# Delta rule on TensorE: square sums as 64x64 products, gate projections after the second T products, diagonal ahead of the cross products

## The chip, the cores and the metric

The kernel runs on one core of one Trainium2 chip. The core has TensorE for matrix products (PE in the profile, its weight loads PEld), VectorE (DVE), ScalarE (ACT), GpSimd (POOL) and SyncE (SP), which issues transfers. Each has its own instruction stream, and they meet through semaphores. All data is fp32, and each product of the program is two matmul records in the trace. The metric is device time in microseconds of the whole program, median of the runs.

## The reference, cut to what matters

The network is eight stages on an input of 8 x 512 x 128. The change is in one of them, the gated delta rule, with 16 heads of 64 channels:

```python
q = (h @ q_w).reshape(bsz, seq, H, DK)      # k and v alike
q = q / (jnp.linalg.norm(q, axis=-1, keepdims=True) + EPS)
k = k / (jnp.linalg.norm(k, axis=-1, keepdims=True) + EPS)
alpha = jax.nn.sigmoid(h @ alpha_w + alpha_b).reshape(bsz, seq, H, DK)
beta = jax.nn.sigmoid(h @ beta_w + beta_b)
def step(s, inp):
    qt, kt, vt, at, bt = inp
    s = s * at[..., None]
    u = jnp.einsum('bhd,bhdv->bhv', kt, s)
    s = s + bt[..., None, None] * (kt[..., None] * (vt - u)[..., None, :])
    out = jnp.einsum('bhdv,bhd->bhv', s, qt)
    return (s, out)
y = y * jax.lax.rsqrt(jnp.mean(y * y, axis=-1, keepdims=True) + EPS) * head_norm_w
```

The square sums of the change are the sums over a head's 64 channels: of q and k for their norms, of y for the last line.

## The kernel before

`stage_delta` works on one batch row and one pair of heads at a time: 8 rows by 8 pairs are 64 steps, and a 65th drains what is behind. Head 0 of a pair lies on partitions 0 to 63, head 1 on 64 to 127. The 512 tokens of a row are 8 chunks of 64. Within a chunk the recurrence is solved by doubling: a triangular matrix T is built over six levels (diagonal blocks of 1, 2, 4, up to 32 tokens, and then the cross blocks between two chunks), and between pairs of chunks a state S is carried.

A step is pipelined over its neighbours. While T of one step is built, the projections, norms and gates of the next step run in between, and so do the output and head norm of the step before. The order is written out by hand for each engine. TensorE has it in `step()` (line 2911), thirteen times in a row in the body of a loop that runs five times:

- `gram(0)`, `cross_z`, `cross_t`, `diagonal`, `gram(1)`, then `solve(0)`, `state_and_output(0)`, `from_state(1)`;
- for the levels 1 to 5: `z_and_gram(l)` (the Z products of level l on two quarters of the array, and the gram products of level l+1 on the other two), VectorE and ScalarE copy one half of Z each (`z_copy`), then `t_step(l)`, and ScalarE copies T (`t_copy`);
- in between `solve(t)`, `state_and_output(t)`, `from_state(t)` for the chunk pairs 1 to 3. ScalarE copies U after each `solve`, and VectorE makes S (`state`) between `state_and_output` and `from_state`;
- of the next step: `project_qk` after `t_step(1)`, `square_sums` after `z_and_gram(2)`, `project_gates` after `z_and_gram(3)`, `key_norms` after `z_and_gram(4)`, `project_v`; of the step before: `head_sums` after `t_step(4)` and `output` after `z_and_gram(5)`.

`square_sums` (line 2839) takes eight products over the whole array: a 128x128 block of squares is the stationary operand and a 128x2 head mask moves. `head_sums` does the same with four.

VectorE has, in its order: `z_copy`, `masked(3)`, `residual(2)`, `sums_in`, `transposed(2)`, `z_copy` of level 3, `norms` (three small operations on the 16 sums, after GpSimd's root), and only then `state(2)`. GpSimd has the gates' multiplications: `carry(l)` multiplies kd and k of level l by tails of alpha and releases `lv_ready`, for which `gram` and `z_and_gram` wait; `roots` is a power of 0.5 over the 16 sums. `gram(1)` waits besides for `gr_free`, which VectorE gives after it has read the gram products of level 0 (`masked(0)`).

Banks of PSUM: Q_ and K_ take the projections, X_ takes the square sums, the diagonal, the key scales and the keys by tokens (`ket`), in turn.

Of the kernel before, what the change touches and what calls it, by code (L numbers as in the profile page):

```python
# [8 lines left out]
ALU = mybir.AluOpType  # L9
# [7 lines left out]
P = 128  # L17
# [2461 lines left out]
def stage_delta(core):  # L2479
# [89 lines left out]
    with nc.Block() as block_:  # L2569
# [12 lines left out]
        def _(g):  # L2582
# [67 lines left out]
            with g.Fori(0, LAST + 1) as i:  # L2650
                ch.reset()
                g.wait_ge(k_free, 1)
                g.sem_clear(k_free)
                carry_k(0, kn)
                carry_kq(0, kd, kdn).then_inc(lv_ready, 1)
# [24 lines left out]
                g.tensor_copy(tH[:], tails(LEVELS + 1)).then_inc(kd_free, 1)  # L2680
# [4 lines left out]
        def _(pe):  # L2685
# [185 lines left out]
            def head_sums():  # L2871
# [38 lines left out]
            pe.sem_inc(out_ps, 1)  # L2910
            def step():
# [52 lines left out]
        def _(a):  # L2964
# [3 lines left out]
            a.sem_inc(ket_ready, 1)  # L2968
# [49 lines left out]
            with a.Fori(0, LAST + 1) as i:  # L3018
                a.wait_ge(kd_free, 1)
# [663 lines left out]
```

## Time and profile before

| | us |
|---|---|
| median of 3 runs | 5245.73 |
| lowest, highest | 5245.05, 5253.82 |
| the profiled execution | 5255.62 |
| its span, from the first to the last instruction | 5253.4 |
| of it, the delta stage's steps | about 1494 to 4005 |
| TensorE busy in the span | 4061.1 (77%) |
| VectorE, ScalarE, GpSimd busy | 2979.3, 1785.2, 2663.1 |

Times of the trace are read from the span's start. A step is measured here from one `e_ZX` copy on ScalarE to the next, since that copy occurs once in each. The share of TensorE's clock that was granted stands in the column PEclk: 1.00 is 2.4 GHz and 0.50 is 1.2 GHz. Matmuls are pipelined, so a group of them ends some 0.1 to 0.2 us after the next one has begun, and what a group costs TensorE is the time from its start to the next one's.

### The profile page before, as it was taken

The page shows a single profiled execution, that of the slowest core. Times are in us where ns is not written, and L with a number is a line of the kernel's source. Part 1 is how long each engine was busy: PE and PEld are TensorE (multiplying, and loading weights), DVE is VectorE, ACT ScalarE, POOL GpSimd, SP SyncE. Part 2 cuts the span into 40 slices and gives each one's busy share as a digit, 9 for nine tenths or more (in the row PEclk, how much of TensorE's full clock was granted, in tenths as well). Part 3 has the DMA queues.
Part 4 walks back from the last instruction along what each step waited for, and adds up shares of the span by engine and source line. Part 5 has one row for each costly group of instructions (what it writes and reads, how often), then busy time and mean ns, then how long its engine had stood idle before and what let it go on. Part 6 is the DMA issues. An engine that isn't in the chain of part 4 may idle for free. (4 is left out here: it accounts for less than half of the span.)

```text
span 5253.4 us, 171720 instructions
## 1 busy us (share of the span) xinstructions
PE 4061.1 (77%) x68604; PEld 3253.1 (62%) x68604; DVE 2979.3 (57%) x8041; ACT 1785.2 (34%) x4061; POOL 2663.1 (51%) x3000
## 2 busy tenths in 40 slices
PE   4679964664179888889898898889897769588685
PEld 2434444553157777777777777767775469577685
DVE  5832277655645655656556565555565554488723
ACT  4722232442023333333333333333333135311163
POOL 2310017514456665666666566666664251377644
PEclk8989986786579998999999999999998879799797
DMA  0030004653000000000000000000000056300154
GB/s 22 3 135 0 0 4 127 184 168 105 15 17 10 13 11 10 13 10 13 11 10 13 11 11 13 11 12 11 11 13 11 1 184 237 109 1 1 58 185 123
DMA packets 129671, 248.79 MB, mean 47 GB/s; under 512 B 24672, under 2 KB 60657, under 8 KB 127345
## 3 DMA queue, kind: packets, MB, share of 16 engines
q1 hardware_dynamic: 98224, 178.93, 10.8%
q0 software_dynamic: 16384, 33.59, 2.2%
q10 hardware_dynamic: 14400, 26.22, 1.4%
q8 instruction: 565, 9.26, 0.7%
q14 instruction: 98, 0.80, 0.0%
HBM read 178.89 MB, written 59.77 MB: 45 GB/s over the span
## 5 line engine op out<-in xcount | busy, mean ns | idle before, releaser
L2596 POOL TENSOR_TENSOR e_kd<-e_kd,e_tail 128x512 f32<-128x512 f32 x325 | 369.1, 1136 | 575.3 <-PE psum L2703 562.8
L2733 PE MATMUL psum<-e_T,e_N 64*64 64x32 f32 x10400 | 403.4, 231 | 65.3 <-remote 63.2
L2733 PEld LDWEIGHTS psum<-e_T,e_N 64*64 64x64 f32 x10400 | 367.3, 147 | 117.9 <-issue 110.5
L2703 PE MATMUL psum<-e_kd,e_k 64*64 64x64 f32 x10400 | 415.7, 235 | 2.3 <-issue 1.7
L729 POOL DMA_INDIRECT m_back<-m_rows_out,m_idx x256 | 254.4, 994 | 302.0 <-DVEq L1169 127.8
L2703 PEld LDWEIGHTS psum<-e_kd,e_k 64*64 64x64 f32 x10400 | 368.3, 147 | 7.3 <-issue 1.1
L723 POOL DMA_INDIRECT rows_in<-xn,m_idx x256 | 256.2, 1001 | 146.2 <-issue 76.2
L2754 PE MATMUL psum<-e_Z,e_TT 64*64 64x32 f32 x8320 | 302.2, 223 | 28.8 <-DVE e_Z L3106 22.6
L840 PE MATMUL psum<-m_rowsT,m_w 128*128 128x128 f32 x2304 | 319.2, 298 | 3.1 <-DVE m_h L1145 2.3
L840 PEld LDWEIGHTS psum<-m_rowsT,m_w 128*128 128x128 f32 x2304 | 306.7, 214 | 5.0 <-DVE m_h L1145 2.3
L3106 DVE COPY e_Z<-psum 64x256 f32<-64x256 f32 x325 | 135.8, 418 | 305.8 <-PE psum L2733 305.6
L2754 PEld LDWEIGHTS psum<-e_Z,e_TT 64*64 64x64 f32 x8320 | 273.7, 137 | 51.3 <-issue 37.8
L2998 ACT ACTIVATE e_T<-psum 128x256 f32<-128x256 f32 x325 | 125.9, 387 | 522.2 <-PE psum L2754 522.2
L856 PE MATMUL psum<-m_wd,m_h 128*128 x1856 | 256.9, 283 | 34.2 <-DVE m_out L1157 31.5
L2590 POOL TENSOR_TENSOR e_k<-e_k,e_tail 128x256 f32<-128x256 f32 x390 | 276.8, 710 | 0.0
L856 PEld LDWEIGHTS psum<-m_wd,m_h 128*128 128x128 f32 x1856 | 235.6, 199 | 39.9 <-issue 39.8
L3005 ACT ACTIVATE e_Z<-psum 64x256 f32<-64x256 f32 x325 | 123.9, 381 | 314.5 <-PE psum L2733 312.9
L384 PE MATMUL psum<-f_hid,f_h 128*128 128x512 f32 x512 | 223.1, 594 | 2.2 <-remote 2.2
L2612 POOL TENSOR_TENSOR e_ssb<-e_ssb,e_half_power 128x16 f32<-128x16 f32 x66 | 191.4, 2899 | 35.6 <-DVE e_ssb L3146 35.6
L818 PE MATMUL psum<-ident,m_rows 128*128 128x128 f32 x400 | 73.5, 314 | 174.8 <-issue 116.0
L3100 DVE COPY_PREDICATED e_AT<-e_lowi,psum 128x256 f32<-128x256 int32 x390 | 205.6, 527 | 0.0
L3113 DVE STREAM_TRANSPOSE e_TT<-e_T 128x512 f32<-128x512 f32 x195 | 138.3, 709 | 102.5 <-ACTq L2999 100.5
(460 smaller groups left out, 10849.6 us busy)
## 6 DMA issues: line engine op xcount, KB each, us to landing
m_w<-in_m_w SPq DMA_DIRECT2D x88, 516.0 KB, 5.8
m_w<-in_m_w SPq DMA_DIRECT2D x224, 129.0 KB, 2.3
m_rows<-rows_in SPq DMA_DIRECT2D x100, 256.0 KB, 3.8
m_rows_out<-m_out ACTq DMA_DIRECT2D x100, 256.0 KB, 2.1
m_w<-in_m_w SPq DMA_DIRECT2D x88, 259.0 KB, 3.7
e_w<-in_e_w SPq DMA_DIRECT2D x66, 321.0 KB, 2.9
rows_in<-xn SPq DMA_DIRECT2D x6, 2048.0 KB, 23.7
m_wd<-in_m_wd SPq DMA_DIRECT2D x3, 2048.0 KB, 8.2
```

The lines of the kernel that those rows point to most:

```text
L384: r = pe.matmul(c.ps[m][:], w[:, k, m * P:(m + 1) * P], hid[n][:, k, :], start=(k == 0), stop=(k == HC - 1))
L723: g.indirect_dma_start(out=xs[i], out_offset=bass.IndirectOffsetOnAxis(ap=idx[i][:, n, k:k + 1], axis=0), in_=y2[:, pl.b0[i] * TB + n, :], ...
L729: g.indirect_dma_start(out=back[:, n, k, :], out_offset=None, in_=os[i], in_offset=bass.IndirectOffsetOnAxis(ap=idx[i][:, n, k:k + 1], axi ...
L840: r = pe.matmul(c.ps[2 * (u % 2) + i][:, cols(j)], w[:, k % WR * BPS + j, n:n + P], xgT[:, k % 2, cols(j)], start=True, stop=True)
L856: r = pe.matmul(c.ps[Y_][:, t * P:(t + 1) * P], h[:, u % DEPTH, t * P:(t + 1) * P], wd[:, bass.ds(experts[0][t // TPB], 1), m * D:(m + 1) ...
L2590: return g.tensor_tensor(even(k[:], m), even(src[:], m), gate, ALU.mult)
L2596: return g.tensor_tensor(both_odd(dst[:], m), both_odd(src[:], m), gate.unsqueeze(1).broadcast_to((P, 2, nb, m)), ALU.mult)
L2612: g.tensor_tensor(flat_ss, flat_ss, half_power[:], ALU.pow).then_inc(root_ready, 1)
L2703: r = pe.matmul(c.psum[half(h), G_, chunk(u)], keys[half(h), chunk(u)], both_odd(gated[half(h), :, chunk(u)], 1 << l), start=True, stop=True)
L2733: r = pe.matmul(c.psum[half(1 - h), Z_, u * HC:(u + 1) * HC], N[half(h), l - 1, chunk(u)], even(T[half(h), chunk(u)], 1 << l), start=True, ...
L2754: r = pe.matmul(even(c.psum[half(h), T_, chunk(u)], 1 << l), left[half(h), chunk(u)], Z[half(h), u, :], start=False, stop=False, skip_grou ...
L3100: return lambda: v.copy_predicated(cols(AT[:]), wide(lowi[:, l, :]), gr[:, :, 1]).then_inc(gr_free, 1)
```

## The change

Four things are moved or rewritten, all in `stage_delta`.

1. `sums_by_head` makes the square sums out of 64x64 products on all four quarters of the array: 32 of them in place of 8 for q and k, 16 in place of 4 for y. The two quarters on the diagonal write to bank X_, the two off it to bank K_, and VectorE adds the two banks: one more small operation in `sums_in` and one more for y. After it has read K_ it gives `sums_read`, for which TensorE waits before it writes K_ again.
2. `project_gates` moves from behind `z_and_gram(3)` to behind `t_step(2)`, ahead of `solve(2)`, and waits for `sums_read` between its two products.
3. `diagonal` goes ahead of `cross_t`. It writes X_, which ScalarE must have read: the copy of `ket` moves from the end of ScalarE's step to the start of the next, behind the copy of k, and the copy of kd moves ahead of the copy of ZX.
4. GpSimd multiplies kd of level 0 first, behind a new semaphore `kd_read` and no longer behind ScalarE's copy of k, and k of level 0 second.

```diff
+            def sums_by_head(of, at, t, done):
+                for bank, other in ((X_, 0), (K_, 1)):
+                    for h in range(2):
+                        a = 1 - h if other else h
+                        r = pe.matmul(c.psum[half(a), bank, 2 * at:2 * at + 2], of[half(h), chunk(2 * t + a)], hm[half(h), :],
+                                      start=True, stop=True)
+                        if done:
+                            r.then_inc(done, 1)
...
-                        at = 2 * (n * TB + t)
-                        r = pe.matmul(c.ps[X_][:, at:at + 2], sq[:, n, block(t)], hm[:], start=True, stop=True)
-                r.then_inc(ss_ps, 1)
+                        sums_by_head(sq[:, n, :], n * TB + t, t, ss_ps if n * TB + t + 1 == 2 * TB else None)
...
-                for n in range(2):
-                    r = pe.matmul(c.ps[Q_ + n][:], W[:, (2 + n) * P:(3 + n) * P], hs[:], start=True, stop=True)
-                r.then_inc(ab_ps, 1)
+                pe.matmul(c.ps[Q_][:], W[:, 2 * P:3 * P], hs[:], start=True, stop=True)
+                pe.wait_ge(sums_read, 1)
+                pe.sem_clear(sums_read)
+                pe.matmul(c.ps[K_][:], W[:, 3 * P:4 * P], hs[:], start=True, stop=True).then_inc(ab_ps, 1)
...
                 for t in range(TB):
-                    r = pe.matmul(c.ps[X_][:, 2 * t:2 * t + 2], ysq[:, block(t)], hm[:], start=True, stop=True)
-                r.then_inc(sy_ps, 1)
+                    sums_by_head(ysq, t, t, sy_ps if t + 1 == TB else None)
 
             def output():
 
+                pe.wait_ge(sums_read, 1)
+                pe.sem_clear(sums_read)
...
-                v.wait_ge(ss_ps, 1)
+                v.wait_ge(ss_ps, 4)
                 v.sem_clear(ss_ps)
-                v.tensor_copy(ssb[:].rearrange("p n t h -> p (n t h)"), c.ps[X_][:, 0:4 * TB]).then_inc(ss_ready, 1)
+                ch.link(v.tensor_copy(sums[:], c.ps[K_][:, 0:4 * TB]))
+                v.sem_inc(sums_read, 1)
+                v.tensor_tensor(ssb[:].rearrange("p n t h -> p (n t h)"), sums[:], c.ps[X_][:, 0:4 * TB], ALU.add).then_inc(ss_ready, 1)
```

On TensorE at the start of a step, `e_T,e_NA` is `cross_z`, `e_TTH,e_ZX` is `cross_t`, `e_kqn,e_kn` is `diagonal` and `e_kd,e_k` is `gram(1)`. Before:

```order
L2764 MATMUL psum<-e_T,e_NA 64x64 x8
L2770 ISA
L2772 ISA
L2775 MATMUL psum<-e_TTH,e_ZX 64x64 x8
L2693 ISA
L2696 MATMUL psum<-e_kqn,e_kn 64x64 x16
L2920 ISA
L2922 ISA
L2709 ISA
L2703 MATMUL psum<-e_kd,e_k 64x64 x16
```

Changed:

```order
L2770 MATMUL psum<-e_T,e_NA 64x64 x8
L2699 ISA
L2702 MATMUL psum<-e_kqn,e_kn 64x64 x16
L2776 ISA
L2778 ISA
L2781 MATMUL psum<-e_TTH,e_ZX 64x64 x8
L2937 ISA
L2939 ISA
L2715 ISA
L2709 MATMUL psum<-e_kd,e_k 64x64 x16
```

The two waits of `cross_t` (the ISA rows ahead of it) now stand behind the diagonal.

On TensorE in the middle of a step, from the square sums (`e_headmask,e_sq`) on; `e_Z,e_TT` is `t_step(2)`, `e_hs,e_w` are the gate projections, `e_bv,..` is `solve(2)` and `e_T,e_N` begins `z_and_gram(3)`. Before:

```order
L2846 MATMUL psum<-e_headmask,e_sq 128x2 x8
L2747 ISA x2
L2750 ISA
L2754 MATMUL psum<-e_Z,e_TT 64x8x4 x16
L2786 ISA
L2788 MATMUL psum<-e_bv,e_TTH 64x64 x2
L2790 MATMUL psum<-e_bv,e_TX 64x64 x2
L2792 MATMUL psum<-e_bv,e_TTH 64x64 x2
L2724 ISA
...
L2703 MATMUL psum<-e_kd,e_k 64x64 x2
L2852 MATMUL psum<-e_hs,e_w 128x512 x2
```

Changed:

```order
L2849 MATMUL psum<-e_headmask,e_sq 64x2 x32
L2753 ISA x2
L2756 ISA
L2760 MATMUL psum<-e_Z,e_TT 64x8x4 x16
L2864 MATMUL psum<-e_hs,e_w 128x512
L2866 ISA
L2867 MATMUL psum<-e_hs,e_w 128x512
L2792 ISA
L2794 MATMUL psum<-e_bv,e_TTH 64x64 x2
L2796 MATMUL psum<-e_bv,e_TX 64x64 x2
L2798 MATMUL psum<-e_bv,e_TTH 64x64 x2
L2730 ISA
```

The gate projections stood behind all of `z_and_gram(3)`, and stand ahead of `solve(2)` now.

On GpSimd at the start of a step, where `e_al` is alpha. Before:

```order
L2653 ISA
L2590 TENSOR_TENSOR e_k<-e_kn,e_al 128x256
L2596 TENSOR_TENSOR e_kd<-e_kdn,e_al 128x512
L2656 COPY e_tail<-e_tailn 128x512
```

Changed:

```order
L2654 ISA
L2597 TENSOR_TENSOR e_kd<-e_kdn,e_al 128x512
L2657 ISA
L2591 TENSOR_TENSOR e_k<-e_kn,e_al 128x256
L2659 COPY e_tail<-e_tailn 128x512
```

The wait for ScalarE's copy of k stood ahead of both multiplications, and stands between them now.

## Rows read from the trace of the kernel before

**Rows 1.** One tile's instructions, ScalarE's ZX copy: min/median/max ns, first and last start

```profile
L3024 ACT ACTIVATE e_ZX<-psum x65: 384/384/386, 1494.0 to 3969.1; 128x256 f32<-128x256 f32 x65
```

**Rows 2.** Five single steps by windows: length, busy by engine, PEclk, DMA share, GB/s

```profile
3121.94:3157.95 36.01, 32.34 (x848) 26.45 (x848) 22.93 (x53) 13.99 (x31) 24.06 (x30) 1.00 0.05 12
3351.40:3388.80 37.40, 33.69 (x848) 27.57 (x848) 22.68 (x53) 13.99 (x32) 24.58 (x30) 0.95 0.05 11
3044.67:3083.27 38.60, 34.98 (x848) 28.02 (x848) 22.65 (x53) 13.99 (x32) 24.11 (x30) 0.91 0.04 11
3194.97:3235.72 40.75, 36.18 (x848) 28.33 (x848) 22.69 (x53) 13.99 (x32) 24.71 (x30) 0.92 0.04 11
1955.68:2001.06 45.38, 37.02 (x848) 29.46 (x848) 23.00 (x54) 13.97 (x31) 26.62 (x32) 0.88 0.04 10
```

**Rows 3.** Windows inside one step, ahead of the clock's fall and behind it

```profile
3082.00:3099.20 17.20, 14.90 (x388) 12.22 (x385) 11.18 (x30) 5.95 (x13) 9.12 (x11) 1.00 0.01 3
3099.20:3106.10 6.90, 6.69 (x110) 4.91 (x107) 2.70 (x6) 0.66 (x2) 4.56 (x3) 0.51 0.01 2
```

**Rows 4.** Timeline of TensorE around that fall: start us, length us, what

```profile
3097.08 1.95 PE L2846 MATMUL psum<-e_headmask,e_sq 128*128 128x2 f32 x16
3098.95 1.68 PE L2754 MATMUL psum<-e_Z,e_TT 64*64 64x32 f32 x32
...
3103.45 3.29 PE L2852 MATMUL psum<-e_hs,e_w 128*128 128x512 f32 x4
```

**Rows 5.** Timeline of TensorE in the undisturbed step of 36.01 us

```profile
3122.59 0.68 PE L2775 MATMUL psum<-e_TTH,e_ZX 64*64 64x64 f32 x16 [0.79 <-DVE e_TTH L3117]
3123.11 1.10 PE L2696 MATMUL psum<-e_kqn,e_kn 64*64 64x64 f32 x32
3124.20 1.15 PE L2703 MATMUL psum<-e_kd,e_k 64*64 64x64 f32 x32
...
3135.69 1.95 PE L2846 MATMUL psum<-e_headmask,e_sq 128*128 128x2 f32 x16
3137.57 1.12 PE L2754 MATMUL psum<-e_Z,e_TT 64*64 64x32 f32 x32
...
3139.59 0.25 PE L2733 MATMUL psum<-e_T,e_N 64*64 64x32 f32 x2 [0.52 <-remote]
...
3140.68 1.98 PE L2852 MATMUL psum<-e_hs,e_w 128*128 128x512 f32 x4
...
3143.70 0.45 PE L2822 MATMUL psum<-e_S,e_kdH 64*64 64x64 f32 x8 [0.32 <-DVE e_S L3125]
...
3151.09 1.05 PE L2878 MATMUL psum<-e_headmask,e_ysq 128*128 128x2 f32 x8
...
3152.15 0.25 PE L2733 MATMUL psum<-e_T,e_N 64*64 64x32 f32 x2
```

**Rows 6.** Timeline of VectorE in the same step

```profile
3122.90 0.73 DVE L3100 COPY_PREDICATED e_AT<-e_lowi,psum 128x256 f32<-128x256 int32 x1
...
3140.88 0.42 DVE L3106 COPY e_Z<-psum 64x256 f32<-64x256 f32 x1 [0.80 <-PE psum L2733]
3141.33 0.78 DVE L3152 TENSOR_SCALAR e_ssb<-e_ssb 128x16 f32<-128x16 f32 x1
3142.15 0.55 DVE L3154 SCALAR_TENSOR_TENSOR e_rq<-e_ssb 128x8 f32<-128x8 f32 x1
3142.62 0.19 DVE L3155 RECIPROCAL e_rk<-e_ssb 128x8 f32<-128x8 f32 x1
3143.26 0.28 DVE L3125 SCALAR_TENSOR_TENSOR e_S<-e_S,e_tH,psum 128x64 f32<-128x64 f32 x1 [0.46 <-PE psum L2802]
```

**Rows 7.** Timeline of GpSimd in the same step

```profile
3122.43 1.50 POOL L2596 TENSOR_TENSOR e_kd<-e_kdn,e_al 128x512 f32<-128x512 f32 x1
...
3138.13 2.90 POOL L2612 TENSOR_TENSOR e_ssb<-e_ssb,e_half_power 128x16 f32<-128x16 f32 x1 [0.41 <-DVE e_ssb L3146]
```

**Rows 8.** Timeline of ScalarE in the same step

```profile
3151.38 0.38 ACT L2998 ACTIVATE e_T<-psum 128x256 f32<-128x256 f32 x1 [1.14 <-PE psum L2754]
```

More of the change, by code:

```diff
@@ L2515, in stage_delta @@
     rq = [st.sb(f"rq{n}", [P, 2 * TB]) for n in range(3)]
-    su = st.sb("su", [P, TB, 2])
+    su, sums = st.sb("su", [P, TB, 2]), st.sb("sums", [P, 4 * TB])
     w_ready, w_free, hs_ready, hs_free = s("w_ready"), s("w_free"), s("hs_ready"), s("hs_free")
     qk_ps, sq_ready, ss_ps, ss_ready, root_ready = s("qk_ps"), s("sq_ready"), s("ss_ps"), s("ss_ready"), s("root_ready")
+    sums_read = s("sums_read")
     rk_ready, rk_ps, ab_ps, al_ready, be_ready = s("rk_ready"), s("rk_ps"), s("ab_ps"), s("alpha_ready"), s("beta_ready")
@@ L2651, in _ @@
                 ch.reset()
+                g.wait_ge(kd_read, 1)
+                g.sem_clear(kd_read)
+                carry_kq(0, kd, kdn)
                 g.wait_ge(k_free, 1)
                 g.sem_clear(k_free)
-                carry_k(0, kn)
-                carry_kq(0, kd, kdn).then_inc(lv_ready, 1)
+                carry_k(0, kn).then_inc(lv_ready, 1)
                 ch.link(g.tensor_copy(tail[:], tailn[:]))
@@ L2679, in _ @@
                 carry_kq(LEVELS, kdH, kd).then_inc(kdh_done, 1)
-                g.tensor_copy(tH[:], tails(LEVELS + 1)).then_inc(kd_free, 1)
+                ch.link(g.tensor_copy(tH[:], tails(LEVELS + 1)))
+                g.sem_inc(kd_free, 1)
+            g.wait_ge(kd_read, 1)
+            g.sem_clear(kd_read)
             g.wait_ge(hs_free, 1)
@@ L2910, in _ @@
             pe.sem_inc(out_ps, 1)
+            pe.sem_inc(ke_ps, 1)
             def step():
@@ L2916, in step @@
                 cross_z()
+                diagonal()
                 cross_t()
-                diagonal()
                 pe.wait_ge(even_ready, 1)
@@ L3018, in _ @@
             with a.Fori(0, LAST + 1) as i:
+                a.wait_ge(ke_ps, 1)
+                a.sem_clear(ke_ps)
+                a.activation(odd(k[:], 1), odd(kn[:], 1), ACT.Copy).then_inc(k_free, 1)
+                a.activation(flat(ket), c.ps[X_][:], ACT.Copy).then_inc(ket_ready, 1)
                 a.wait_ge(kd_free, 1)
                 a.sem_clear(kd_free)
-                a.activation(odd(k[:], 1), odd(kn[:], 1), ACT.Copy).then_inc(k_free, 1)
+                a.activation(both_even(kd[:], 1), both_even(kdn[:], 1), ACT.Copy).then_inc(even_ready, 1)
                 a.wait_ge(zx_ps, 1)
@@ L3061, in _ @@
                 t_copy(5)
[L3062 to L3064 removed]
+            a.wait_ge(ke_ps, 1)
+            a.sem_clear(ke_ps)
             a.wait_ge(kd_free, 1)
             a.sem_clear(kd_free)
+            a.sem_inc(ket_ready, 1)
         @block_.vector
@@ L3238, in _ @@
                 values(i + 1)
-                v.wait_ge(sy_ps, 1)
+                v.wait_ge(sy_ps, 4)
                 v.sem_clear(sy_ps)
-                v.scalar_tensor_tensor(su[:].rearrange("p t h -> p (t h)"), c.ps[X_][:, 0:2 * TB], 1.0 / DH, rq[0][:],
-                                       ALU.mult, ALU.add).then_inc(su_ready, 1)
+                ch.link(v.scalar_tensor_tensor(sums[:, 0:2 * TB], c.ps[K_][:, 0:2 * TB], 1.0 / DH, rq[0][:], ALU.mult, ALU.add))
+                v.sem_inc(sums_read, 1)
+                v.scalar_tensor_tensor(su[:].rearrange("p t h -> p (t h)"), c.ps[X_][:, 0:2 * TB], 1.0 / DH,
+                                       sums[:, 0:2 * TB], ALU.mult, ALU.add).then_inc(su_ready, 1)
                 transposed(4)
```

12 lines of the change are left out of this document (4 added, 8 removed).

## Prediction

> **What bounds the kernel now.** The change touches only the delta stage, so I read how long one of its 65 steps takes and how much that varies. The first and the last ZX copy [rows 1] are 3969.1 - 1494.0 = 2475.1 us apart, 64 steps of 38.67 us on average. The windows over single steps [rows 2] show three kinds. A step whose granted clock is 1.00 takes 36.01 us, one in which the clock is low for a while 37.40, one in which it is low for twice as long 38.60; rarer are one with two falls (40.75) and the step in which the loop jumps back (45.38, 6.8 more than 38.60; there are four of these, 27 us, and I leave them as they are). Without them the mean is 38.67 - 27 / 64 = 38.25, so 2.24 us of an average step is the low clock.
>
> In the undisturbed step TensorE is busy for 32.34 of 36.01 us, and VectorE for 22.93, ScalarE for 13.99, GpSimd for 24.06 [rows 2]: TensorE bounds it, and what isn't TensorE's own work is a row of short waits of 0.3 to 0.8 us [rows 5]. The clock falls behind the square sums [rows 3, 4]. Up to 3099.20 it is granted in full, although the 16 records that move two columns each have just run for 1.95 us without a gap; then it is 0.51 for 6.9 us, the second T products take 1.68 instead of 1.12, and the gate projections 3.29 instead of 1.98 [rows 4, 5]. TensorE was not idle before the fall, it was doing little per unit of time.
>
> The Trainium skill ("TensorE: Matmul & The Clock Gate", "Why this matters for your kernels") ties the fall to idle gaps between bursts of matmuls. The rows above show a fall with TensorE busy throughout, so here the trace does not follow that reading.
>
> **Start of the step (parts 3 and 4).** Today `cross_t` waits 0.79 us for the ZX copy, `diagonal` follows, and `gram(1)` starts at 3124.20 [rows 5]. That start is GpSimd's doing: its kd of level 0 ends at 3122.43 + 1.50 = 3123.93 [rows 7]. The change puts the diagonal into the wait, so that TensorE could be 0.79 earlier, and takes GpSimd out of last place, since the 1.50 us multiplication no longer waits for ScalarE. Next in line is `gr_free`: VectorE's masked copy of level 0 ends at 3122.90 + 0.73 = 3123.63 [rows 6], nothing in the change moves it, and from a VectorE end to the product that waits takes 0.16 (S ends at 3143.54, `from_state` starts at 3143.70 [rows 5, 6]). So `gram(1)` starts at 3123.79: **0.4 us** gained of the 0.79. The copies moved on ScalarE fill its idle time ahead of ZX; if they made ZX late, that would fall behind the diagonal (1.10 us).
>
> **Square sums (part 1).** Today 16 records take 3137.57 - 3135.69 = 1.88 us. Afterwards they are 64 records on four quarters with two columns moving. The trace has no such group. The nearest is `z_and_gram`, 64 records on four quarters with 32 or 64 columns moving: 3140.68 - 3139.59 = 1.09 us [rows 5]. The bounds: no cheaper than half of that if the columns counted, no dearer than today's 1.88. I take 1.09, for the same number of 64x64 weight loads: gain **0.79 us**, range 0 to 1.3. The extra addition on VectorE costs at most 0.2 us (the smallest operation there is 0.19 [rows 6]) and lies ahead of GpSimd's root, which starts 0.5 us earlier or more anyway because the sums do.
>
> By the Trainium skill ("TensorE: Matmul & The Clock Gate", "LDWEIGHTS") a load takes its columns over 1.2 per ns, 53 ns for 64; sixteen in each quarter would be an estimated 0.85 us, and the gain 1.03 instead of 0.79. In the rows `z_and_gram` takes 1.09, and the rows decide.
>
> **Gate projections (part 2).** They add nothing; they move. They now cover the wait for the copy of T, 0.52 us ahead of `z_and_gram(3)` [rows 5], and `sums_read` between them costs nothing, since VectorE reads the sums during the T products (1.12). But they covered something where they stood: with 1.98 us between `z_and_gram(3)` and `state_and_output(2)` VectorE had time for its Z copy and the norms before `state(2)`. Follow this in the clean step. `z_and_gram(3)` starts at 3139.59 - 0.40 - 0.79 - 0.52 + 1.98 = 3139.86, so 0.27 later than today. VectorE's Z copy starts 1.29 behind it (3140.88 - 3139.59 [rows 5, 6]): 3141.15 to 3141.57. The norms take 1.48 (3141.33 to 3142.81 [rows 6]) to 3143.08; the root they need takes 2.90 on GpSimd and ends at 3141.03 today [rows 7], earlier afterwards. S takes 0.28, and `from_state(3)` starts at about 3143.55, where it starts at 3143.70 today [rows 5]. Of 1.71 us gained up to there **0.15** is left; `state_and_output(2)` comes 1.98 sooner after `z_and_gram(3)` than it did, and TensorE stands idle for about 2 us behind it, waiting for S. With roundings in my favour (0.1 us less for the square sums, which need no change of tiling behind them) it may be 0.25.
>
> **Head sums.** Eight records at 1.05 become 32 records, by the same rate half of 1.09. `z_and_gram(5)`, next, starts today at 3152.15, which is also when T is there: its copy ends at 3151.38 + 0.38 = 3151.76 [rows 8], and 0.39 from T copy to product is what it takes. So of 0.5 us at most 0.1 counts. `output` now waits for `sums_read`, covered by `z_and_gram(5)`.
>
> **Sum, clock apart.** 0.15 to 0.35 us a step, I take 0.3, times 64 is 19 us.
>
> **The clock.** 2.24 us a step is at stake, 143 us in all. In favour: the thin stretch shrinks from 1.88 to 1.09 us; and a fall behind it would now spend about 2 of its 6.9 us on idle time, where a halved clock costs nothing: 2.24 x 2 / 6.9 = 0.65 us. Against: the idle stretch is itself a new place at which the clock may fall. I take half of the 0.65, 0.35 us a step, 22 us. Together 41 us: the profiled execution's 5255.62 becomes 5215. It lies 9.9 over the median of the runs, so for the median I say 5245.7 - 41 = **5205**.
>
> **The rivals.**
> - *The clock hardly falls any more.* With the thin stretch cut nearly in half most steps run at 35.7 (36.01 - 0.3), a third with a fall of 1.4 (37.40 - 36.01 [rows 2]): 36.2. That is 38.25 - 36.2 = 2.05 x 64 = 131 us at best and half of that if every step keeps one short fall (37.1: 74 us). Middle: 5143. For: undisturbed steps exist today with the long thin stretch. Against: the new idle stretch. 0.2.
> - *The stall takes it all.* `from_state(3)` starts where it did, the falls stay as they are: 5235 to 5256. For: my own sum leaves 0.15 of 1.71. 0.13.
> - *Slower: a second fall in each step.* The 2 us of idle TensorE behind `state_and_output(2)` bring the clock down besides the fall behind the square sums. A step with two falls costs 40.75 - 36.01 = 4.74 [rows 2]; at about 4 a step takes 35.7 + 4 = 39.7, 1.45 x 64 = 93 us more: 5338; if it happens in every third step, 5270. It decides once the low clock costs over 2.54 us a step. Against: waits of 0.8 us pass without a fall [rows 5], but none of 2 us is in the rows. 0.1. The page of the Trainium skill cited above, on idle gaps, speaks for this rival.
> - *Slower: two-column products don't gain from the quarters.* If 64 small records take 1.88 again, `z_and_gram(3)` starts 1.06 later than today, `from_state(3)` 0.6: 0.5 x 64 = 32 us slower, 5275. It decides from 1.5 us. Against: `z_and_gram`. 0.07.
>
> **How the numbers follow.** My forecast, 5190 to 5230, has 0.5. Below it lies the clock rival (0.2), above it the stall (0.13), the two slower ones (0.17). The range 5125 to 5270 leaves out the best of the first and most of the slower ones, about 0.17. A measurement tells 0.2% apart, 10.5 us: faster 0.5 + 0.2 and a little of the stall rival: 0.73; same 0.11; slower 0.16.
>
> **What would show it.** In the changed profile: `diagonal` straight behind `cross_z`, and `gram(1)` 0.4 earlier against ZX, released by VectorE. 64 square sum records in 1.0 to 1.1 us; 1.5 or more makes that step wrong. An idle time of about 2 us ahead of `from_state(3)`, released by VectorE's S, with the three norm operations straight ahead of it. Undisturbed steps of 35.6 to 35.8; under 35.3 would mean that the stall is smaller than I reckon, over 36.0 that it is larger. And the spread: the share of steps with a low clock, whether it falls behind the square sums or behind the idle stretch. A PEclk of 0.94 in the stage as a whole would mean no gain from the clock, and if it went under 0.9, the prediction is wrong in sign.

## The result, and the profile after

| | before | after |
|---|---|---|
| median of 4 runs each, us | 5245.39 | 5305.01 |
| lowest, highest | 5236.94, 5253.82 | 5300.68, 5310.45 |
| the profiled execution | 5255.62 | 5310.45 |
| 64 steps of the delta stage | 2475.1 | 2524.95 |
| an undisturbed step | 36.0 | 35.4 |

The ratio is 1.0114, 95% interval 1.0095 to 1.0133: 60 us slower, where 41 us faster was forecast. The two profiled executions are 55 us apart, and 50 of these lie in the 64 steps. Windows over the stage and over single steps (length; busy time and instructions of PE, PEld, DVE, ACT, POOL; PEclk, DMA share, GB/s), first the stage before:

```profile
1494.00:3969.10 2475.10, 2206.07 (x54272) 1787.33 (x54272) 1452.37 (x3328) 895.12 (x1984) 1559.78 (x1854) 0.94 0.04 11
```

and then the changed kernel, its stage and four of its steps [rows 2]:

```profile
1499.14:4024.09 2524.95, 2125.72 (x58886) 1714.12 (x58884) 1424.78 (x3457) 883.45 (x1985) 1530.47 (x1855) 0.92 0.04 11
2948.86:2984.25 35.39, 30.32 (x927) 25.05 (x924) 22.14 (x55) 13.80 (x32) 23.92 (x30) 1.00 0.05 13
2791.91:2829.52 37.61, 31.88 (x927) 25.91 (x924) 22.24 (x55) 13.80 (x32) 23.95 (x30) 0.95 0.04 12
2829.52:2868.23 38.71, 31.95 (x928) 25.48 (x924) 22.22 (x55) 13.80 (x32) 23.91 (x30) 0.96 0.04 11
3069.11:3112.47 43.36, 36.57 (x928) 28.96 (x924) 22.35 (x55) 13.83 (x32) 23.98 (x30) 0.84 0.04 11
```

TensorE has 80 us less work in the stage, the undisturbed step is 0.6 us shorter, and the stage is longer all the same. So the loss is in what disturbs the steps. One part of that are falls of the granted clock to half. The clock record says how often: stretches at half clock, called low clock from here on, add up to 315 us before and 399 after (PEclk 0.94 and 0.92 are the same thing: 1 - 315 / (2 x 2475) and 1 - 399 / (2 x 2525)). 7 of 64 steps had two falls before, 20 have two or more now, and 4 have none, where 11 had.

TensorE in the undisturbed step [rows 5], from its timeline (start, length, line, tiles, idle time before it and who ended it):

```profile
2948.65 1.03 PE L2702 MATMUL psum<-e_kqn,e_kn 64*64 64x64 f32 x29
2949.52 0.68 PE L2781 MATMUL psum<-e_TTH,e_ZX 64*64 64x64 f32 x16
2950.71 1.15 PE L2709 MATMUL psum<-e_kd,e_k 64*64 64x64 f32 x32 [0.51 <-DVE e_AT L3120]
...
2961.24 0.25 PE L2739 MATMUL psum<-e_T,e_N 64*64 64x32 f32 x2
...
2962.19 1.09 PE L2849 MATMUL psum<-e_headmask,e_sq 64*64 64x2 f32 x64
2963.24 1.12 PE L2760 MATMUL psum<-e_Z,e_TT 64*64 64x32 f32 x32
2964.30 1.12 PE L2864 MATMUL psum<-e_hs,e_w 128*128 128x512 f32 x2
2965.26 1.02 PE L2867 MATMUL psum<-e_hs,e_w 128*128 128x512 f32 x2
...
2970.29 0.45 PE L2828 MATMUL psum<-e_S,e_kdH 64*64 64x64 f32 x8 [2.02 <-DVE e_S L3145]
...
2973.85 1.08 PE L2874 MATMUL psum<-e_sq,e_ones 128*64 128x512 f32 x4
...
2977.35 0.63 PE L2849 MATMUL psum<-e_headmask,e_ysq 64*64 64x2 f32 x30
```

The diagonal fills the wait for ZX, `gram(1)` starts 1.85 us behind ZX in place of 2.26 and is released by VectorE, and the square sums take 1.05 us up to the next group. And there is an idle stretch of 2.02 us ahead of `from_state(3)`. VectorE in that stretch [rows 6]:

```profile
2967.80 0.42 DVE L3126 COPY e_Z<-psum 64x256 f32<-64x256 f32 x1 [2.04 <-PE psum L2739]
2968.25 0.78 DVE L3174 TENSOR_SCALAR e_ssb<-e_ssb 128x16 f32<-128x16 f32 x1
2969.06 0.54 DVE L3176 SCALAR_TENSOR_TENSOR e_rq<-e_ssb 128x8 f32<-128x8 f32 x1
2969.53 0.19 DVE L3177 RECIPROCAL e_rk<-e_ssb 128x8 f32<-128x8 f32 x1
2969.86 0.28 DVE L3145 SCALAR_TENSOR_TENSOR e_S<-e_S,e_tH,psum 128x64 f32<-128x64 f32 x1
```

The three norm operations stand between the Z copy and S, and TensorE waits for S.

**What comes behind the idle stretch.** The step of 37.61 us by windows: up to 2816.30, the 3.4 us behind that, and TensorE's idle stretch by itself:

```profile
2791.91:2816.30 24.39, 19.50 (x569) 15.31 (x564) 15.30 (x41) 6.60 (x16) 15.25 (x18) 1.00 0.01 3
2816.30:2819.70 3.40, 3.02 (x68) 2.10 (x68) 1.19 (x3) 1.76 (x4) 2.04 (x6) 0.50 0.00 0
2812.14:2814.16 2.02, 0.00 (x0) 0.01 (x1) 1.85 (x5) 0.00 (x0) 2.02 (x3) 1.00 0.00 0
```

TensorE idles until 2814.16 and the clock halves at 2816.3. Where in a step do the falls begin? Before, 51 falls began behind the square sums (between 12 and 21.7 us after ZX) and none behind `from_state(3)` (21.7 to 29.5 us). Now 32 begin behind the sums and 45 behind `from_state(3)`. The others, 9 before and 5 now, begin 9.7 to 10.8 us after ZX or past 37.

**What happens to the square sums.** In the step of 38.71 us they read otherwise:

```profile
2842.83 0.57 PE L2849 MATMUL psum<-e_headmask,e_sq 64*64 64x2 f32 x27
2845.01 0.65 PE L2849 MATMUL psum<-e_headmask,e_sq 64*64 64x2 f32 x33 [1.61 <-issue]
2845.53 1.12 PE L2760 MATMUL psum<-e_Z,e_TT 64*64 64x32 f32 x32
```

TensorE stops in the middle of a group whose operands are all there, for 1.61 us, and "issue" says that nothing in the profile was waited for. The line's own page counts what this costs in the whole program, in the matmul queue:

```profile
L2849 PE MATMUL psum<-e_headmask,e_sq x4224: 161/194/262, 1480.0 to 4040.2; 64*64 64x2 f32 x192
...
  issue: 49.9, 30
```

30 pauses and 49.9 us; 29 of them fall into the 64 steps. Before, the 66 groups had one such wait (3.8 us). The pauses have an order: in each of the three whole passes of the loop that I counted, they fall into the steps 1, 3, 6, 8, 10 and 12 of the 13, and all pauses inside groups of small products, these and others, fall on TensorE's instruction number 242 or 243 modulo 256, counted from the loop's start (matmuls, weight loads and semaphore instructions as recorded). The kernel before has such pauses as well, at 82 to 85 modulo 256, but only 4.3 us of them in 13 steps, where the changed kernel has 14.6. The instruction queue's row of the DMA section over the stage, before and after:

```profile
q8 instruction: 448, 7.34, 1.3%
```

```profile
q8 instruction: 481, 7.88, 1.3%
```

A packet is 7.34 MB / 448 = 16.4 KB. The loop body of 13 steps is 22880 and 24780 recorded TensorE instructions, so the 64 steps of these windows are 440 and 477 times 256, against 448 and 481 packets. So nearly all of this queue is TensorE's program, 256 instructions in a packet. Around the pause above the DMA view of 2841 to 2845, 40 slices of 0.1 us, shows one packet:

```profile
GB/s 0 0 0 0 0 0 0 0 0 0 0 0 0 0 0 0 0 164 0 0 0 0 0 0 0 0 0 0 0 0 0 0 0 0 0 0 0 0 0 0
...
q8 instruction: 1, 0.02, 1.5%
```

It moves at 2842.7, and the group goes on at 2845.01. The other pauses look the same: the changed kernel has 60 pauses of over 0.25 us inside groups of equal products between its first and last ZX copy, and each ends 2.2 to 2.9 us after the start of the packet before it, while the packets come 5.1 us apart in the median. From the start of `z_and_gram(2)` to the end of the quarter sums TensorE uses up 256 instructions (64 products and 64 weight loads each) in 2.0 us (2961.24 to 2963.24 in the undisturbed step), less than these 2.2 to 2.9 us from packet to instruction.

### The profile page after: what moved, and what is told of

Same layout as the page of the kernel before. It is cut to its first block and busy times, and to the rows that moved or that the text cites. A ratio compares the mean times of both kernels' runs of the same rounds, so it can differ in the third digit from the quotient of the medians.

```text
span 5308.5 us, 181702 instructions
## 1 busy us (share of the span) xinstructions
PE 3979.9 (75%) x73332; PEld 3179.5 (60%) x73332; DVE 2952.3 (56%) x8172; ACT 1773.6 (33%) x4061; POOL 2630.0 (50%) x3000
## 5 line engine op out<-in xcount | busy, mean ns | idle before, releaser
L2760 PE MATMUL psum<-e_Z,e_TT 64*64 64x32 f32 x8320 | 315.8, 227 | 36.1 <-DVE e_Z L3126 21.1
L2760 PEld LDWEIGHTS psum<-e_Z,e_TT 64*64 64x64 f32 x8320 | 290.2, 143 | 54.5 <-issue 46.4
L2591 POOL TENSOR_TENSOR e_k<-e_k,e_tail 128x256 f32<-128x256 f32 x390 | 253.9, 651 | 0.0
L2828 PE MATMUL psum<-e_S,e_kdH 64*64 64x64 f32 x1560 | 89.2, 233 | 171.8 <-DVE e_S L3145 171.8
L3028 ACT ACTIVATE e_U<-psum 128x128 f32<-128x128 f32 x260 | 71.7, 276 | 402.3 <-PE psum L2798 389.9
```

The costliest lines, as they stand in the source:

```text
L2591: return g.tensor_tensor(even(k[:], m), even(src[:], m), gate, ALU.mult)
L2760: r = pe.matmul(even(c.psum[half(h), T_, chunk(u)], 1 << l), left[half(h), chunk(u)], Z[half(h), u, :], start=False, stop=False, skip_grou ...
```

## The experiments

Each kernel is the changed kernel with one edit, unless it says otherwise. Low clock is the sum of half-clock stretches in the 64 steps, in us; pauses are those inside groups, in us per 13 steps. A ratio is against the kernel before on the same chip.

| run | ratio, 95% interval | 64 steps, us | shortest step | low clock | pauses |
|---|---|---|---|---|---|
| kernel before | 1 | 2475 | 35.99 | 315 | 4.3 |
| changed kernel | 1.0114 (1.0095, 1.0133) | 2525 | 35.37 | 399 | 14.6 |
| e1_full_sums | 1.0052 (1.0038, 1.0065) | 2489 | 37.14 | 332 | 2.3 |
| e2_sums_only | 0.9996 (0.9981, 1.0011) | 2471 | 35.50 | 266 | 15.5 |
| e3_start_only | 0.9892 (0.9868, 0.9915) | 2402 | 35.44 | 246 | 2.5 |
| e4_norms_late | 0.9829 (0.9805, 0.9854) | 2377 | 34.45 | 192 | 13.4 |
| e6_fill_aligned | 0.9838 (0.9816, 0.9859) | 2383 | 35.19 | 85 | 7.8 |
| e7_fill_drift | 0.9960 (0.9945, 0.9976) | 2434 | 35.61 | 144 | 13.3 |
| e8_full_norms_late | 0.9830 (0.9808, 0.9852) | 2383 | 34.98 | 201 | 3.1 |
| e9_norms_late_unroll65 | 0.9843 (0.9814, 0.9872) | 2387 | 34.45 | 188 | 15.8 |
| e10_wide_norms_late | 0.9735 (0.9713, 0.9757) | 2332 | 34.40 | 69 | 14.5 |
| e11_wide_only | 1.0022 (1.0006, 1.0037) | 2474 | 35.47 | 294 | 13.3 |
| e12_full_wide_norms_late | 0.9734 (0.9717, 0.9752) | 2318 | 35.16 | 45 | 2.8 |
| e13_before_wide | 0.9830 (0.9809, 0.9851) | 2373 | 35.99 | 59 | 3.2 |
| e14_shift128 | 1.0124 (1.0095, 1.0152) | 2545 | 35.43 | 403 | 15.1 |
| e15_shift64 | 1.0150 (1.0133, 1.0168) | 2556 | 35.36 | 413 | 16.2 |

The last three ran on chips on which the kernel before takes 5586.41 (e13) and 5563.56 us (e14, e15). Their traces reach the first of the 64 steps at 1635 to 1643 us, where the others do at 1480 to 1500, so much of what is longer there lies ahead of the delta stage, and only ratios and stage times compare with the rest. Stage, low clock and pauses come from one profiled execution each; that of e12 took 5081.22 us, 22 below its median.

A shortest step isn't always an undisturbed one. e1's is its only step without low clock and holds a pause of 1.16 us, so without it 36.0:

```profile
2233.77 0.32 PE L2798 MATMUL psum<-e_bv,e_TTH 64*64 64x64 f32 x2 [1.16 <-issue]
```

e6's follows a step of 41.9 us, and e8's and e12's are the first of the stage; the next shortest without low clock take 35.46, 35.18 and 35.29.

**Taking the change apart.** e1 puts the full-array sums back and leaves parts 2 to 4; e2 is the kernel before with part 1 alone; e3 is the kernel before with parts 3 and 4 alone.

```diff
-                        sums_by_head(sq[:, n, :], n * TB + t, t, ss_ps if n * TB + t + 1 == 2 * TB else None)
+                        at = 2 * (n * TB + t)
+                        r = pe.matmul(c.ps[X_][:, at:at + 2], sq[:, n, block(t)], hm[:], start=True, stop=True)
```

> The changed kernel with the square sums and head sums as full-array products again (part 1 undone; gates, diagonal and GpSimd order as changed). Theory A (TensorE starves for instructions: in the changed kernel pauses of 0.6 to 2 us stand at every recorded index 242 modulo 256 that falls into dense small products, 15 us per 13 steps, against 3 to 5 us before): without the 64-record groups the long pauses inside the sums go, pauses fall to under 5 us per 13 steps, undisturbed steps get longer (about 36.0 to 36.4, since the sums take 1.88 and the norms stall behind z_and_gram(3) stays), and the time is 5240 to 5275, faster than the changed kernel's 5305. Theory B (the 2 us idle stretch ahead of from_state(3) lowers the clock and is the whole loss): the idle stretch stays, so low-clock time stays near 400 us and the time stays at 5300 or rises to 5330.

> The kernel before with part 1 alone (square sums and head sums on quarters of the array, gates, diagonal and GpSimd order as before). Theory A (starving for instructions): pauses of 1 to 2 us inside or behind the 64-record group in 4 to 7 of 13 steps, all at one index modulo 256; undisturbed steps about 35.3 to 35.6, mean step 38.5 to 39.3, time 5240 to 5290. Theory B (idle stretch): no 2 us idle ahead of from_state(3) here, so the group's 0.8 us is pure gain: 5190 to 5215.

> The kernel before with parts 3 and 4 alone (diagonal ahead of the cross products, GpSimd's kd first). Both theories: gram(1) 0.4 us earlier in each step, nothing else new: undisturbed steps 35.6, about 25 us faster than before, 5220, as long as pauses at block ends stay at 3 to 5 us per 13 steps. If the time is over 5240, the 0.4 us is taken back by the clock or by new places of the pauses.

Measured medians: 5272.34, 5239.92 and 5186.87 us, the kernel before 5240.35. e1 lies in theory A's range and e2 at its lower edge, both outside theory B's. Part 1 alone is worth nothing: the shortest step is 0.49 us shorter, and the pauses go from 4.3 to 15.5 us in 13 steps, 0.86 us a step. Parts 3 and 4 alone are worth 53 us, more than the 25 expected. From e3 to e1 only the gate projections move: 85 us slower, low clock 246 to 332, and the undisturbed step goes from 35.44 to about 36.0. 55 of e1's falls begin behind `from_state(3)`, where e3 has none. So part 2 as written costs about 35 us in the step, and 86 us more of low clock, which cost at most 43, are most of the rest. From e1 to the changed kernel the quarter sums come on top: 33 us slower.

**The idle stretch.** e4 puts VectorE's norms behind `residual(3)`, so that S no longer stands behind them. e6 leaves them and puts 35 small products of no use into the idle stretch (their result is overwritten), so many that a step has 2048 instructions and the packets' bounds lie at the same places in each; e7 puts 24, and the bounds go on drifting.

```diff
-                norms()
                 ...
                 residual(3)
+                norms()
```

```diff
+            def fill(n):
+
+                for j in range(n):
+                    h = j % 2
+                    pe.matmul(c.psum[half(h), O_, 3 * P:3 * P + DH], eye[half(h), :], eye[half(h), :], start=True, stop=True,
+                              skip_group_check=True)
...
                 z_and_gram(3)
                 state_and_output(2)
+                fill(35 + extra)
                 from_state(3)
```

(`extra` is 6 in the first of 13 steps and 0 in the others.)

> The changed kernel with VectorE's three norm operations moved from ahead of state(2) to behind residual(3). Theory B (idle stretch): the 2 us idle ahead of from_state(3) shrinks to under 0.5, key_norms waits up to 1 us more, undisturbed steps 34.6 to 35.0, low-clock time falls from 400 to under 330 us, time about 5215 to 5250. Theory A: pauses at index 242 modulo 256 stay at about 15 us per 13 steps, and the time gains only what the undisturbed step gains, 0.5 us a step: 5265 to 5285.

> The changed kernel with 35 more 64x64 products (140 instructions, six more once per 13 steps; their result is overwritten and unused) between state_and_output(2) and from_state(3), where TensorE idles for 2 us. A step becomes 2048 instructions, so that the ends of 256-instruction blocks fall at the same places in every step, one of them inside z_and_gram(2), none inside the square sums. Both causes are taken away: theory A expects pauses of under 4 us per 13 steps instead of 15; theory B expects no fall of the clock behind the idle stretch, low-clock time under 250 us instead of 400. The stall itself stays, undisturbed steps 35.4 to 35.6. Both right: 5150 to 5200. Only A right: about 5255. Only B right: about 5230.

> As the aligned one, but with 24 added products (96 instructions), so that block ends drift by 46 instructions a step and still fall into the square sums in some steps. Theory A: pauses of 8 to 16 us per 13 steps remain, the time lies 25 to 50 us above the aligned kernel. Theory B: the clock behaves as in the aligned kernel (under 270 us of low clock). If the two kernels come out alike, the pauses don't matter.

Measured: e4 5161.73, e6 5163.44, e7 5226.84 us. e4 in TensorE's timeline of its shortest kind of step, and VectorE ahead of it:

```profile
2890.22 0.45 PE L2828 MATMUL psum<-e_S,e_kdH 64*64 64x64 f32 x8 [0.41 <-DVE e_S L3145]
```

```profile
2889.33 0.42 DVE L3126 COPY e_Z<-psum 64x256 f32<-64x256 f32 x1 [2.04 <-PE psum L2739]
2889.78 0.28 DVE L3145 SCALAR_TENSOR_TENSOR e_S<-e_S,e_tH,psum 128x64 f32<-128x64 f32 x1
```

The idle time goes from 2.02 to 0.41 us, the shortest step from 35.37 to 34.45, and the falls behind `from_state(3)` from 45 to none. 0.92 x 64 = 59 us is the shorter step, and the other 84 of the 143 us gained come with the low clock, 399 to 192 us, and some 6 us of pauses. The gain is more than either theory had expected. e6 has the idle stretch filled and no shorter way through the step, which has 2.33 us of added work,

```profile
2844.75 2.33 PE L2932 MATMUL psum<-e_eye 64*64 64x64 f32 x70
2846.94 0.45 PE L2828 MATMUL psum<-e_S,e_kdH 64*64 64x64 f32 x8
```

and is 142 us faster than the changed kernel, with low clock 399 to 85 us. That is two things at once: of the 142 us some 33 are pauses, 14.6 to 7.8 us in 13 steps, which is half and not the under 4 that was expected. e7 keeps the pauses nearly as they were (13.3) and shows the filling nearly by itself: 78 us faster than the changed kernel, low clock 399 to 144 us, and 2 falls behind `from_state(3)` in place of 45. It is 63 us slower than e6, more than the 25 to 50 expected. 5.5 us in 13 steps, 27 us in 64, are pauses, and it has 59 us more of low clock: 23 falls behind the square sums, where e6 has 15. Its 24 products also leave 0.62 us idle ahead of `from_state(3)` in most steps, where e6 leaves none, so the pair does not separate the pauses cleanly from the filling.

**Full sums and late norms; no loop jump.** e8 is e1 with late norms, e9 is e4 with all 65 steps written out and no loop.

> The changed kernel with full-array square and head sums and with VectorE's norms behind residual(3). If the quarter products are worth their pauses once the idle stretch is gone, this is slower than the norms-late kernel with quarter sums (5162): undisturbed steps 0.8 longer (35.3) and 10 us per 13 steps of pauses less, that is the same within 10 us, 5150 to 5175. If the thin stretch of full-array sums still brings the clock down in most steps, 5180 to 5210.

> The norms-late kernel (quarter sums) with TensorE's 65 steps written out instead of a loop of five times thirteen. The four steps with the jump back cost about 6.8 us more each, so 27 us go: 5135. Theory A: blocks now are 16 KB pieces of one straight stream, so the pauses come at one index modulo 256 again but in other steps, about 1 us a step as before. If the jump back costs nothing by itself, 5162.

Measured: 5163.49 and 5170.91 us. e8 against e4 (5161.73) is the square sums once more, 1.9 us of 16 large products against 1.1 us of 64 small ones: the same time. Its steps without low clock take mostly 35.2 to 35.3 us, 0.8 longer than e4's 34.5, and 0.8 us a step of pauses are gone. e9 missed the 5135 that it would take if each jump cost 6.8 us, and gained nothing on e4: its longest steps take 40.6 us, where e4 has four of 41.9 to 44.4 at the loop's jumps, and the pauses are 15.8 us in 13 steps for 13.4.

**What the clock falls behind.** e4 and e8 have no idle stretch and still fall, 33 and 40 times, behind the square sums. In e10 to e13 the head mask is 64 columns wide, 62 of them zero; number and size of the weight loads stay, and VectorE picks the two useful columns of each 64.

```diff
-    ones, hm = st.sb("ones", [P, DH]), st.sb("headmask", [P, 2])
+    ones, hm = st.sb("ones", [P, DH]), st.sb("headmask", [P, DH])
...
-                        r = pe.matmul(c.ps[X_][:, at:at + 2], sq[:, n, block(t)], hm[:], start=True, stop=True)
+                        r = pe.matmul(c.ps[X_][:, at:at + DH], sq[:, n, block(t)], hm[:], start=True, stop=True)
```

> The changed kernel with VectorE's norms behind residual(3) (as in the earlier run with the late norms, 5161.73 us), and with a head mask of 64 columns in place of 2, 62 of them zero: each of the quarter products of the square sums and the head sums moves 64 columns, the number of products and of weight loads stays. Theory A (with the idle stretch gone, the falls that are left come behind the group of two-column products): the low clock in the 64 steps goes from 192 us to under 100, and the time to 5100 to 5135. Theory B (the falls that are left come from elsewhere, the pauses in TensorE's instruction stream for one): the square sums take 1.1 us still, the pauses about 13 us in 13 steps, the low clock stays at 150 to 230 us and the time within 15 us of 5162. Against both: if 64 columns in fp32 cost more than 2, the square sums take over 1.3 us and the undisturbed step is longer than 34.45.

> The changed kernel (5305.0 us) with the head mask of 64 columns alone; the norms stay where the change has them, so that the idle 2 us ahead of from_state(3) stay. If the idle stretch is where the low clock comes from, it stays at 350 us or more of 399, and the time within 20 us of 5305. If the two-column products are, the low clock goes under 250 us and the time under 5240.

> The run with full-array square sums and late norms (5163.5 us, low clock 201 us, undisturbed step 34.98) with the mask of 64 columns: 16 records that move 64 columns each in place of 2. Theory A (falls come behind the two-column products, more so behind 1.9 us of them than behind 1.1): low clock under 100 us, and the time 5110 to 5140 if the group still takes 1.9 us. Theory B: low clock 170 to 230 us, and 5150 to 5180.

> The kernel before with the mask of 64 columns alone (62 of them zero); the order of the work stays the kernel before's, full-array square sums, 16 records that move 64 columns each in place of 2. If the group of two-column products is what the clock falls behind there (as the windows and the timeline of TensorE around a fall were read in the prediction), the low clock in the 64 steps goes from 315 us to under 150, and the time from 5246 to 5150 or less, with the undisturbed step still near 36.0 to 36.4. If the falls are only met there by chance and come from elsewhere, it stays over 250 us and the time at 5225 to 5255.

Measured: e10 5112.37, e11 5256.27, e12 5103.58, the kernel before 5244.52; e13 5484.46, the kernel before on its chip 5586.41. e10, e12 and e13 came out by the theory of the two-column products, e12 some 6 us below its range. The stages of e10, e12 and e13 by windows:

```profile
1499.98:3832.26 2332.28, 2005.20 (x58888) 1630.98 (x58886) 1450.83 (x3456) 883.94 (x1985) 1554.85 (x1854) 0.99 0.05 12
```

```profile
1479.51:3797.47 2317.96, 2066.10 (x54280) 1705.29 (x54279) 1434.49 (x3328) 882.55 (x1985) 1556.28 (x1854) 0.99 0.05 12
```

```profile
1634.88:4007.51 2372.63, 2098.84 (x54272) 1716.70 (x54272) 1454.44 (x3328) 895.39 (x1984) 1557.95 (x1854) 0.99 0.05 12
```

PEclk 0.99 in all three. In the kernel before the 51 falls behind the square sums (in its trace, from another chip) become one in e13, with nothing but 62 columns of zeros added, and the program is 102 us faster than the kernel before on the same chip. With quarter sums the zeros help and don't cure: of e4's 33 falls behind the sums e10 keeps 10. e12 has none there and loses its clock only at the loop's jumps and in a few others, 7 steps in all. The wider mask costs next to nothing: the group in e13 and in e10,

```profile
2985.20 2.00 PE L2846 MATMUL psum<-e_headmask,e_sq 128*128 128x64 f32 x16
2987.13 1.12 PE L2754 MATMUL psum<-e_Z,e_TT 64*64 64x32 f32 x32
```

```profile
2862.88 1.15 PE L2849 MATMUL psum<-e_headmask,e_sq 64*64 64x64 f32 x64
2864.01 1.12 PE L2760 MATMUL psum<-e_Z,e_TT 64*64 64x32 f32 x32
```

takes 1.93 in place of 1.88 us, and 1.13 in place of 1.05. The Trainium skill has this ("TensorEngine Tiling (Array Packing)", "Instruction Overhead"): a matmul that moves one column takes as long as one that moves about 60. The rows agree within 0.08 us a group.

e11 came out between its two theories, low clock 294 where under 250 or over 350 was expected: 17 falls are left behind the sums, where the changed kernel has 32, and 48 behind the idle stretch, where it has 45. Both are causes, and they add up: late norms alone gain 143 us on the changed kernel, the wide mask alone 49, both together 193 (e10).

**The pauses.** e14 and e15 put 32 and 16 small products, 128 and 64 recorded instructions, ahead of the loop. Inside the loop nothing is changed.

```diff
+            for j in range(32):
+                h = j % 2
+                pe.matmul(c.psum[half(h), O_, 3 * P:3 * P + DH], eye[half(h), :], eye[half(h), :], start=True, stop=True,
+                          skip_group_check=True)
             pe.sem_inc(out_ps, 1)
             pe.sem_inc(ke_ps, 1)
```

> The changed kernel with 32 small products (128 recorded instructions on TensorE) ahead of the loop of the 65 steps, their result overwritten; nothing inside the loop is changed. Theory P (the pauses of 0.6 to 2 us inside the groups of small products are TensorE running out of instructions, which come in packets of 256): the pauses move by 128 instructions, from index 242 or 243 modulo 256 of the loop's body to about 114, and the square sums pause in the steps 0, 2, 9, 11 modulo 13 (and 5, 7 perhaps) and run through in 1, 3, 6, 8, 10, 12, where they pause now. Rival Q (something else with the period of the loop, memory traffic or another engine, stops TensorE there): they stay in the steps 1, 3, 6, 8, 10, 12. Both: the time within 25 us of 5305.

> The same with 16 small products (64 recorded instructions). Theory P: pauses at index 178 or 179 modulo 256; that index falls near the start of the square sums (steps 1, 3, 5, 7, 8, 10, 12), where full-sized work stands ahead, so that packets are in time more often and the pauses cost 5 to 12 us in 13 steps in place of 14.6; the time 5260 to 5310. Rival Q: as the kernel without the shift, pauses in steps 1, 3, 6, 8, 10, 12 at index 242 or 243.

Measured: 5641.39 and 5647.88 us, the kernel before 5563.56. The pauses moved to 113 and 114, and to 177 and 178 modulo 256, and the square sums pause in the steps 0, 2, 5, 7, 9, 11 of e14 and 1, 3, 5, 7, 10, 12 of e15, as theory P had it but for one step (8) of e15. Two neighbouring steps of the changed kernel, numbers 9 and 10 modulo 13:

```profile
2882.46 1.09 PE L2849 MATMUL psum<-e_headmask,e_sq 64*64 64x2 f32 x64
```

```profile
2920.62 0.86 PE L2849 MATMUL psum<-e_headmask,e_sq 64*64 64x2 f32 x45
2923.19 0.51 PE L2849 MATMUL psum<-e_headmask,e_sq 64*64 64x2 f32 x19 [1.71 <-issue]
```

and the same two in e14, where they have changed places:

```profile
3051.53 0.74 PE L2849 MATMUL psum<-e_headmask,e_sq 64*64 64x2 f32 x38
3053.80 0.62 PE L2849 MATMUL psum<-e_headmask,e_sq 64*64 64x2 f32 x26 [1.52 <-issue]
```

```profile
3091.83 1.09 PE L2849 MATMUL psum<-e_headmask,e_sq 64*64 64x2 f32 x64
```

So where the pauses fall hangs on where in the instruction stream a group stands; nothing in the step itself was changed. That e15 would have fewer of them was a miss: 16.2 us in 13 steps against 14.6, and its ratio of 1.0150 is above the range expected too. Shifting doesn't cure it. Fewer instructions in a dense stretch bring the pauses to 2.3 to 3.1 us (e1, e3, e8, e12), and bounds that stay out of the square sums to 7.8 (e6).

**A pause brings a fall with it.** The traces show one thing more when the steps are sorted by whether the square sums hold a pause. Steps with a fall behind the sums:

| run | with a pause in the sums | without |
|---|---|---|
| kernel before | none has one | 51 of 64 |
| changed kernel | 25 of 29 | 7 of 35 |
| e2_sums_only | 29 of 29 | 20 of 35 |
| e4_norms_late | 25 of 29 | 8 of 35 |
| e6_fill_aligned | none has one | 15 of 64 |
| e7_fill_drift | 15 of 21 | 8 of 43 |
| e10_wide_norms_late | 9 of 30 | 1 of 34 |

In the changed kernel the clock falls between 0.3 us before the pause ends and 2.5 us after. So the pauses cost more than their own length, and the shorter group did avert falls where no pause lay in it. That the pause is the cause rests on these counts and on e6, where the packets' bounds stay out of the sums. No run changes the pauses in the sums alone.

## Why the prediction was wrong

- **Start of the step: right.** 0.41 us against 0.4, released by VectorE. e3 has it alone and gains 53 us in all, of which 0.55 x 64 = 35 are the shorter step.
- **Square sums: right in the group, wrong as a cost.** 1.05 us to the next group, forecast 1.09. But in 29 of 64 steps it holds a packet's bound and its records begin over 2.4 to 3.4 us in place of 0.9. Over the stage the pauses grew by (14.6 - 4.3) x 64 / 13 = 51 us, and the whole 0.83 x 64 = 53 us that the quarters gain went there. e10 and e12, which differ in the quarters alone, end within 9 us of each other. The prediction took 64 records of `z_and_gram` as the measure of 64 records here; a group's price alone left out what a dense stretch asks of the instruction supply. The sum had no term for it, and no row ahead of the result shows one. The kernel before has pauses too (4.3 us in 13 steps, 0.33 us a step), and the prediction counted them among the 2.24 us of low clock.
- **Gate projections: right in the path.** `from_state(3)` starts 21.43 us behind ZX in place of 21.76, so 0.33 earlier (forecast 0.15 to 0.25), with 2.02 us idle ahead of it, the three norms in it, released by S.
- **The undisturbed step** is 0.62 us shorter, forecast 0.3. 0.33 of it is there at `from_state(3)`. Then `t_step(3)`, which starts 0.66 us behind `from_state(3)` in the kernel before and 0.50 now, adds 0.16:

```profile
3144.36 1.12 PE L2754 MATMUL psum<-e_Z,e_TT 64*64 64x32 f32 x32
```

```profile
2970.79 1.07 PE L2760 MATMUL psum<-e_Z,e_TT 64*64 64x32 f32 x32
```

  At `key_norms` it is 0.54 (24.99 us behind ZX in place of 25.53). The head sums, for which at most 0.1 was forecast, give the last 0.08: they end 0.7 us after they begin in place of 1.05, but TensorE then waits 0.46 us for VectorE, and `z_and_gram(5)` starts 29.59 us behind ZX in place of 30.21:

```profile
2978.45 0.25 PE L2739 MATMUL psum<-e_T,e_N 64*64 64x32 f32 x2 [0.46 <-DVE e_AT L3120]
```

  So what the sum lacked is the stretch between `from_state(3)` and `z_and_gram(4)`, and why it shrank stays open.
- **The clock: wrong, and this is the step that failed, next to the pauses.** The prediction took 0.35 us a step, 22 us, as gained; about 39 were lost. The low clock grew from 315 to 399 us. Of the 50 us by which the stage is longer, -40 are the shorter step (0.62 x 64) and +51 the pauses, so 39 are left, and 84 us more at half clock cost at most 42. The term "against", the idle stretch as a new place to fall, was named and then priced at nothing; taking the stretch away in e4 gives 84 us beside the shorter step. That a fall would be spent in part on idle time, the reason for the gain, didn't hold either: the fall comes behind the idle stretch, at 2816.3 where it ended at 2814.16, and of all the low clock 24.5 us lay on idle time of TensorE before and 16.5 do now. Of the 32 falls that are still behind the sums 25 are in steps where the sums hold a pause.
- **The rivals.** The second fall was the right mechanism for half of the loss, at 0.1. It came in about a third of the steps (20 with two or more, of which 7 were there before). For every third step the rival said 5270; that the time lies between this and its 5338 is partly luck, since the pauses, which it hadn't, add as much again. The Trainium skill's page cited there ("TensorE: Matmul & The Clock Gate", "Why this matters for your kernels") is borne out by e4 and e7 as to idle stretches between bursts, though it speaks of longer ones than the 2.02 us here, and by e13 it isn't the whole: in the kernel before, falls come with no idle time ahead of them, and go when the same products move 64 columns. Reading the falls behind the square sums as theirs [rows 3, 4] was right, and "the thin stretch shrinks from 1.88 to 1.09 us" was half a remedy: without a pause the short stretch has 7 falls in 35 steps (changed kernel), where the long one has 51 in 64, but with one it has 25 in 29, and e2 still has 49 in all. e13 has the long stretch, with zeros, and one fall.

The two best kernels are e12 (5103.58 us, 2.7% faster than before) and e10 (5112.37), too close to be told apart. e12 keeps parts 2 to 4, with full-array sums, the wide mask and the late norms.

## What to carry to other kernels

When work is moved that covered a wait, ask who used the cover: here VectorE's norms did, and moving them too turned 1% slower into 1.7% faster. Where the clock falls behind products that move two columns, let them move 64, with zeros, before splitting them up: in the kernel before that cost 0.05 us in the group and took 50 of 51 falls away. And count instructions where small products are dense: a rewrite that quadruples them can give back in pauses, and in the falls that come with them, what it gains in products, and the sign of it is idle time by "issue" inside a group, at a fixed instruction number modulo 256.

## What the runs showed of the hardware

- TensorE stops for up to 2.1 us inside groups of small products where a 16 KB packet of its instructions, 256 of them, comes late. All 60 pauses of over 0.25 us in the changed kernel end 2.2 to 2.9 us after the start of a packet. Instructions put ahead of the loop move the pauses by exactly their number (242 to 114 and 178).
- 62 zero columns in the moving operand of the square and head sums of the kernel before (128x128 products) left the group at 1.93 us for 1.88, and PEclk over the 64 steps is 0.99, where the kernel before has 0.94.
- In the changed kernel the clock falls behind the square sums in 25 of 29 steps with such a pause in them, and in 7 of 35 without.
- An idle stretch of 2.02 us of TensorE in each step goes with 45 falls of the clock behind it in 64 steps; filled with 24 useless products it has 2 falls, and the program is 78 us faster.
